# Layer 2 of a four-layer image network on one NeuronCore: three buffers in its first and last pass, ACT and PSUM in the first, and padded rows of delta*u in DRAM

## The reference

```
xc    = silu(conv3x3(x_norm @ in_proj_w[:, :C]) + conv_b);  z = the other half
xs    = [xc in row order, reversed, in column order, reversed]        # 4 directions
proj  = xs @ x_proj_w                                                 # 12 + 16 (B) + 16 (C) rows
delta = softplus(proj[:12] @ dt_w + 2 * dt_b)
state = exp(delta * A) * state + (delta * u) * B                      # per channel, 16 states, 3136 steps
y     = sum over states(state * C) + D * u
out   = x + (layernorm(sum of the 4 directions) * ln_g + ln_b) * z @ out_w
```

## Time and profile before

| what | value |
|---|---|
| time, median of 3 runs | 19143.47 us (19140.31 to 19148.17) |
| profiled execution, its own time | 19173.11 us |
| its span, first to last instruction | 19171.4 us |
| busy share PE, PEld, DVE, ACT, POOL | 78, 58, 61, 38, 36% |
| DMA | 2640.22 MB, mean 138 GB/s |
| mean granted TensorE clock | 0.794 |

### The profile page before, as it was taken

One profiled execution on the slowest core, in us unless ns is written; L12 is line 12 of the kernel. 1 busy time (PEld: TensorE's weight loads), 2 busy tenths in 40 slices (PEclk: granted clock), 3 DMA queues, 4 the chain that ended last, 5 costly groups with the idle time before them and its releaser, 6 DMA issues. The chain is left out here.

```text
span 19171.4 us, 359393 instructions
## 1 busy us (share of the span) xinstructions
PE 14991.3 (78%) x130080; PEld 11045.3 (58%) x130080; DVE 11710.9 (61%) x10632; ACT 7349.9 (38%) x12681; POOL 6928.4 (36%) x3199
## 2 busy tenths in 40 slices
PE   7899898989997534444888888888888888854489
PEld 5666666666665211122777677767777677732267
DVE  5666666666665666565667676667677667732232
ACT  4444444444443333333444444444444444411100
POOL 1000000000000233335777677767777677721100
PEclk9999999999998766676777777777777777765699
DMA  5222222222223555657999999899889999954411
GB/s 123 58 59 59 63 54 59 59 63 59 59 53 89 130 139 139 149 133 171 209 208 210 211 209 208 207 210 209 207 209 211 208 210 210 210 129 115 115 48 40
DMA packets 1692801, 2640.22 MB, mean 138 GB/s; under 512 B 1081676, under 2 KB 1245260, under 8 KB 1667404
## 3 DMA queue, kind: packets, MB, share of 16 engines
q1 hardware_dynamic: 1680332, 2551.26, 56.3%
q0 software_dynamic: 12288, 86.71, 2.1%
HBM read 2110.03 MB, written 556.32 MB: 139 GB/s over the span
## 5 line engine op out<-in xcount | busy, mean ns | idle before, releaser
L1680 DVE TENSOR_TENSOR_SCAN L2.h<-L2.ps,L2.db 128x912 f32<-128x912 f32 x2688 | 5514.0, 2056 | 2416.1 <-POOL L2.db L1545 2320.6
L1545 POOL TENSOR_TENSOR L2.db<-L2.du,L2.bt 128x896 f32<-128x896 f32 x2688 | 5576.7, 2093 | 2388.2 <-DMA L2.du<-du 2306.2
L1568 PE MATMUL L2.ps<-L2.dm,L2.wa 32*128 32x112 f32 (+2 forms) x24192 | 4522.0, 346 | 1132.1 <-DVE L2.h L1680 1005.5
L1568 PEld LDWEIGHTS L2.ps<-L2.dm,L2.wa 32*128 32x128 f32 x24192 | 4169.2, 258 | 1838.8 <-DVE L2.h L1680 1294.7
L1620 ACT ACTIVATE L2.ps<-L2.ps 128x896 f32<-128x896 f32 x2688 | 2426.0, 903 | 4607.2 <-PE L2.ps L1568 4606.8
L1580 PE MATMUL L2.ps<-L2.h,L2.cd 128*8 128x96 f32 x50176 | 2575.8, 362 | 4.2 <-DVE L2.h L1680 4.2
L1580 PEld LDWEIGHTS L2.ps<-L2.h,L2.cd 128*8 128x8 f32 x50176 | 1443.6, 108 | 583.8 <-DVE L2.h L1680 4.3
L1137 POOL TENSOR_TENSOR L2p.work<-L2p.work,L2p.xc 128x784 f32<-128x784 f32 x192 | 451.3, 2350 | 1659.2 <-DVE L2p.work L1300 1659.2
L314 POOL TENSOR_TENSOR L1.x_res<-L1.x_res,L1.ob 96x3136 f32 (+1 forms) x16 | 95.4, 5976 | 2584.8 <-ACT L1.qv L457 2584.8
L366 PE MATMUL L1.p_proj<-L1.xt,L1.w_hi 128*96 128x448 f32 x3024 | 826.9, 383 | 194.3 <-DVE L1.xt L560 167.4
L366 PE MATMUL L0.p_proj<-L0.xt,L0.w_hi 128*96 128x448 f32 x3024 | 824.2, 382 | 193.9 <-DVE L0.xt L560 167.4
(11 more groups left out here) (242 smaller groups left out, 20801.6 us busy)
## 6 DMA issues: line engine op xcount, KB each, us to landing
L2.du<-du SPq DMA_DIRECT2D x2688, 448.0 KB, 11.1
L2.dm<-d SPq DMA_DIRECT2D x896, 336.0 KB, 10.8
du<-L2p.work SPq DMA_DIRECT2D x128, 784.0 KB, 7.6
y<-L2.ysum SPq DMA_DIRECT2D x896, 84.0 KB
L0.left<-table SPq DMA_DIRECT2D x48, 1176.0 KB
L0.right<-table SPq DMA_DIRECT2D x48, 1176.0 KB
L1.left<-table SPq DMA_DIRECT2D x48, 1176.0 KB
L1.right<-table SPq DMA_DIRECT2D x48, 1176.0 KB
```

Of the source, the lines that this page charges most:

```text
L1545: pool.tensor_tensor(db[:, n % RB, :, 2:ROW], du[:, n % RD, :].rearrange("p (c t) -> p c t", t=SPAN), row, ALU.mult)\
L1568: mm = pe.matmul(decays[n % RA][:, a:b], wa[rows, j, :], dm[rows, j, a - lo:b - lo], start=True, stop=True)
L1680: dve.tensor_tensor_scan(h[:, half, u * UNIT:(u + 1) * UNIT, :].rearrange("p c t -> p (c t)"), decays[n % RA], db[:, n % RB, :, :].rearran ...
```

## The change

In `prep_layer`: `one` and `d` get a third buffer, which lies in `xn` parts 0 and 1, and `hi` a second, in `xn` part 2. `one_of(n)` and `d_of(n)` choose by (n + 1) % 3, `hi_of(n)` by (n + 1) % 2. ACT's logarithm writes to `ln_out`, one buffer of two PSUM banks, so that logarithm q waits for DVE's subtraction of q - 1; the copy to hi moves from DVE to ACT, between the logarithms. The next pair's `load_x` moves from before the tiles to after the stores of tile 10, and waits until they have landed. In `fin_layer`: three buffers; SP loads only y, as soon as the turns of the chunk three before are done, and ahead of the stores; ACT issues the loads of xc, z and x; PE's order becomes `skips(i + 1)`, `turns(i)`, `shares(i - 1)`, and DVE's `total(i + 1)`, `gate(i)`, `add_out(i - 1)`. In DRAM each (image, copy) of `du` becomes one flat row with `UNIT * SPAN` = 896 floats behind it, 3584 bytes; its stores and loads address the same data in it. The semaphores and counts follow.

```diff
+        ones = [work[:, (1 + s) * TOK:(2 + s) * TOK] for s in range(2)] + [xn[:, 0, :]]
+        ds = [work[:, (3 + s) * TOK:(4 + s) * TOK] for s in range(2)] + [xn[:, 1, :]]
+        his = [hi[:], xn[:, 2, :].bitcast(F32R)]
         pads = [v.rearrange("p (h w) -> p h w", w=PADDED)
                 for v in (pad0[:], work[:, TOK:TOK + PADDED * PADDED], work[:, 3 * TOK:3 * TOK + PADDED * PADDED])]
...
-        def d_stores(n, step=1):
+        def one_of(n):
+
+            return ones[(n + 1) % 3]
+
+        def d_of(n):
+
+            return ds[(n + 1) % 3]
+
+        def hi_of(n):
+
...
-                    sp.wait_ge(d_step, 2 * q)
+                    sp.wait_ge(hi_done, q)
                     for run in set_runs(pr, i):
-                        store_part(0, hi[:].bitcast(F32), *run).then_inc(hi_stored[half], 16)
+                        store_part(0, hi_of(n).bitcast(F32), *run).then_inc(hi_stored[n % 2][half], 16)
                     sp.wait_ge(du_done, q)
                     for at, b, c, size in runs(pr, i):
                         for copy in range(COPIES):
-                            sp.dma_start(du_dram[k, b, copy, spans, c:c + size, :].rearrange("s c t -> c s t"),
-                                         one[n % 2][at:at + size, span].rearrange("p (s t) -> p s t", t=SPAN))\
-                                .then_inc(du_stored[n % 2][half], 16)
+                            rows = du_dram[k, b, copy, 0:NSPANS * CH * SPAN].rearrange("(s c t) -> c s t", c=CH, t=SPAN)
+                            sp.dma_start(rows[c:c + size, spans, :],
+                                         one_of(n)[at:at + size, span].rearrange("p (s t) -> p s t", t=SPAN))\
+                                .then_inc(du_stored[n % 3][half], 16)
                     sp.wait_ge(lo_done, q)
                     for run in set_runs(pr, i):
-                        store_part(1, d[n % 2], *run).then_inc(lo_stored[n % 2][half], 16)
+                        store_part(1, d_of(n), *run).then_inc(lo_stored[n % 3][half], 16)
             load_x(0)
...
-                if pr + 1 < PAIRS:
-                    load_x(pr + 1)
                 for i in range(3):
...
                         store_rows(pr, j // 3 + 1)
+                    if j == TILES - 2 and pr + 1 < PAIRS:
+                        n = pr * TILES + j
+                        for half in range(2):
+                            sp.wait_ge(hi_stored[n % 2][half], d_stores(n + 2, 2))
+                            sp.wait_ge(lo_stored[n % 3][half], d_stores(n + 3, 3))
+                            sp.wait_ge(du_stored[n % 3][half], du_stores(n + 3, 3))
+                        load_x(pr + 1)
...
-                    if n >= 2 and q % 2 == 0:
-                        act.wait_ge(lo_stored[n % 2][q // 2], d_stores(n, 2))
+                    if n >= 3 and q % 2 == 0:
...
             def log(pr, j):
                 n = pr * TILES + j
+
+                def split(q):
+                    act.wait_ge(d_step, 4 * n + q + 1)
+                    if n >= 2 and q % 2 == 0:
+                        act.wait_ge(hi_stored[n % 2][q // 2], d_stores(n, 2))
+                        act.wait_ge(lo_done, 4 * (n - 2) + q + 2)
+                    act.copy(hi_of(n)[:, piece(q)], d_of(n)[:, piece(q)]).then_inc(hi_done, 1)
+
                 for q in range(4):
                     act.wait_ge(s_step, 12 * n + 3 * q + 2)
-                    act.activation(one[n % 2][:, piece(q)], one[n % 2][:, piece(q)], ACT.Ln).then_inc(ln_done, 1)
+                    if n or q:
+                        act.wait_ge(d_step, 4 * n + q)
+                    act.activation(ln_out, one_of(n)[:, piece(q)].rearrange("p (a n) -> p a n", a=2), ACT.Ln)\
+                        .then_inc(ln_done, 1)
+                    if q:
+                        split(q - 1)
+                split(3)
             for pr in range(PAIRS):
                 act.wait_ge(step, pr * STEPS + 9)
...
                 for q in range(4):
-                    o_q, d_q = (v[n % 2][:, piece(q)] for v in (one, d))
+                    d_q = d_of(n)[:, piece(q)].rearrange("p (a n) -> p a n", a=2)
                     dve.wait_ge(ln_done, 4 * n + q + 1)
                     dve.wait_ge(s_step, 12 * n + 3 * q + 3)
-                    dve.scalar_tensor_tensor(out=d_q, in0=o_q, scalar=ln1[:], in1=d_q, op0=ALU.subtract,
+                    dve.scalar_tensor_tensor(out=d_q, in0=ln_out, scalar=ln1[:], in1=d_q, op0=ALU.subtract,
                                              op1=ALU.add).then_inc(d_step, 1)
-                    dve.wait_ge(d_step, 8 * n + 2 * q + 1)
-                    if n and q % 2 == 0:
-                        dve.wait_ge(hi_stored[q // 2], d_stores(n))
-                        dve.wait_ge(lo_done, 4 * (n - 1) + q + 2)
-                    dve.tensor_copy(hi[:, piece(q)], d_q).then_inc(d_step, 1)
             def conv(pr, i):
...
             def load_du(k, s, half, u):
                 c = half * HALF + u * UNIT
-                rows = du_dram[k].rearrange("b o s c t -> (b o) s (c t)")
+                rows = du_dram[k, :, :, 0:NSPANS * CH * SPAN].rearrange("b o (s n) -> (b o) s n", s=NSPANS)
...
-        yk = m.sb("yk", [SPAN, 2, DIRS, LINES, CH])
...
+        NS = 3
+        yk = m.sb("yk", [SPAN, NS, DIRS, LINES, CH])
...
                                 sp.dma_start(place_e[SIDE * a:SIDE * a + SIDE], src).then_inc(y_in[s], 16)
-                span = slice(t * CHUNK, (t + 1) * CHUNK)
-                sp.dma_start(xc[:, s, :, :], xc_dram[pr, :, :, span]).then_inc(xc_in[s], 16)
-                sp.dma_start(zc[:, s, :, :], z_dram[pr, :, :, span]).then_inc(fin_in[s], 16)
-                for out, src in image_parts(x_in, pr, lambda i: xr[:, s, i, :], t * CHUNK, CHUNK):
-                    sp.dma_start(out, src).then_inc(fin_in[s], 16)
-
-            load(0)
-            load(1)
-            for n in range(NC):
-                s = n % 2
+
+            def store(n):
                 sp.wait_ge(out_done, n + 1)
-                for src, dst in image_parts(x_out, n // NCHUNK, lambda i: oc[:, s, i, :], n % NCHUNK * CHUNK, CHUNK):
-                    sp.dma_start(dst, src).then_inc(x_stored[s], 16)
-                if n + 2 < NC:
-                    load(n + 2)
-            for s in range(2):
-                sp.wait_ge(x_stored[s], 64 * NC // 2)
+                for src, dst in image_parts(x_out, n // NCHUNK, lambda i: oc[:, n % NS, i, :], n % NCHUNK * CHUNK, CHUNK):
+                    sp.dma_start(dst, src).then_inc(x_stored[n % NS], 16)
+
+            for n in range(NS):
+                load_y(n)
+            for i in range(NC + 1):
+                if i + NS < NC:
+                    sp.wait_ge(turned, 3 * (i + 1))
+                    load_y(i + NS)
+                if i:
+                    store(i - 1)
+            for s in range(NS):
+                sp.wait_ge(x_stored[s], 64 * len(range(s, NC, NS)))
         @block.gpsimd
         def _(pool):
             for n in range(NC):
...
             skips(0)
-            for n in range(NC):
-                turns(n)
-                if n + 1 < NC:
-                    skips(n + 1)
-                shares(n)
+            for i in range(NC + 1):
+                if i + 1 < NC:
+                    skips(i + 1)
+                if i < NC:
+                    turns(i)
+                if i:
+                    shares(i - 1)
...
+            def load_xc(n):
+                pr, t = divmod(n, NCHUNK)
+                if n >= NS:
+                    act.wait_ge(skip_ready, (n - NS + 1) * (LINES // 2))
+                act.dma_start(xc[:, n % NS, :, :], xc_dram[pr, :, :, t * CHUNK:(t + 1) * CHUNK]).then_inc(xc_in[n % NS], 16)
+
+            def load_z(n):
+                pr, t = divmod(n, NCHUNK)
+                if n >= NS:
+                    act.wait_ge(gated, n - NS + 1)
+                act.dma_start(zc[:, n % NS, :, :], z_dram[pr, :, :, t * CHUNK:(t + 1) * CHUNK]).then_inc(z_in[n % NS], 16)
+
+            def load_x(n):
+                if n >= NS:
+                    act.wait_ge(out_done, n - NS + 1)
+                for out, src in image_parts(x_in, n // NCHUNK, lambda i: xr[:, n % NS, i, :], n % NCHUNK * CHUNK, CHUNK):
+                    act.dma_start(out, src).then_inc(xr_in[n % NS], 16)
+
+            for n in range(NS):
+                load_xc(n)
+            for n in range(2):
+                load_z(n)
...
+            for i in range(NC):
+                scale(i)
+                if i + 1 < NC:
+                    normalise(i + 1)
+                if i + NS < NC:
+                    load_xc(i + NS)
+                if i + 2 < NC:
+                    load_z(i + 2)
+                if i + 1 < NC:
+                    load_x(i + 1)
         @block.vector
...
+            def gate(n):
+
+                s = n % NS
                 dve.wait_ge(scaled, 3 * n + 3)
-                dve.wait_ge(fin_in[s], 80 * (n // 2 + 1))
+                dve.wait_ge(z_in[s], 16 * (n // NS + 1))
```

(24 more changed lines are left out.)

106 lines of the change are left out of this document (53 added, 53 removed).

## The result

| | before | after |
|---|---|---|
| median | 19142.56 us (4 runs, 19140.31 to 19148.17) | 18094.31 us (4 runs, 18079.56 to 18105.79) |
| ratio | | 0.9451, 95% interval 0.9438 to 0.9463 |
| profiled execution | 19173.11 us | 18079.56 us |
| first pass | 2724.7 | 2303.1 |
| scan | 7952.0 | 7952.2 |

A stage is counted here from its first DMA on the SP queue (the first pass from its second, the load of `w_gn`) to the next stage's first. So counted, the last pass took 1344.9 us before; the 1375 of the earlier trace rows reach 30 us into layer 3. The change brings 1048 us (5.5%); forecast were 1090.

The account below looks back on a forecast made before the run. Stores alternating with arithmetic were taken to bound the first pass, a circle of loads, work and stores the last; in the scan DMA was 0.90 busy. Terms -450 - 640 + 0 = -1090 gave 18050 us, range 16950 to 18450.

Parts of the forecast that it names:

- First pass, -450 forecast: First pass of layer 2: a direction falls from 134.2 to 104 us, 16 times, less 30 for the moved load.
- The step from the stores to ACT's order: First pass: with third buffers, stores need 86 us a direction, ACT's program order 104, so ACT becomes the bound.
- factor 16: First pass: the gain per direction, 134.2 - 104 us, counted for all 16 directions, 483 us.
- load of `x`: First pass, pair changes: the later load is mostly covered by tile 11's arithmetic; 10 us per pair, 30 in all.
- the 3.00 of my upper end: First pass: DVE's subtraction at 3.00 us beside POOL instead of 1.03, giving 128 us a direction.
- Last pass, -640 forecast: Last pass: three buffers and the new order overlap loads with work, a chunk falls from 49.1 to 25 us.
- lower end of 21.6 us a chunk: Last pass: DMA bound if the clock rises with denser PE work, 735 us off.
- that rule alone: Last pass: issuing from more engines saves only issuing time, 4.6 us a chunk, 130 us in all.
- Scan, 0 forecast: Scan: the changed pitch of du has no effect, 35.5 us a half span and 209 GB/s stay; chance 0.60.
- padding works: Rival, chance 0.25: in the scan the pad lifts du loads from 271 to 387 GB/s, 960 us off, 17090 in all.
- padding hurts: Rival, chance 0.04: in the scan the pad drops du loads to 203 GB/s, 1520 us on, 19570 in all.
- the lone unit's 387 GB/s: Scan: one du load alone at the old pitch reaches 387 GB/s, so its aligned rows do not collide.

Follow-up runs that it names:

- spreading the copies: Copies to f, with PE's projections, dealt out in pairs around the soft parts of two tiles, against the changed kernel: 17947.3 us, first pass 2163.0.
- distinct pieces: Scan loads of delta*u read 128 different DRAM pieces instead of 16 pieces 8 times each, against the changed kernel: 18038.5 us, scan 7906.0.

## Why the prediction was right, and where it wasn't

**The whole.** 18050 was forecast, 18094 came, inside the range. In the profiled executions the stages give -421.6 + 0.2 - 669.2 = -1090.6, against -1090; the medians differ by 1048, since the profiled execution of before lay 30 us above its median and that of after 15 us below. That the stages' sum met the forecast within 1 us is luck: the first pass brought 28 us less than forecast and the last 29 more.

**First pass, -450 forecast, -421.6 measured.** The step from the stores to ACT's order as the bound was right, and spreading the copies showed it. The direction came out at 100.3 instead of 104: soft 11.0 as in the earlier trace rows, log 10.7 without the long wait (10.2 forecast), copies 28.2 (25), and waits of 2 x 3.8 instead of 15. (134.2 - 100.3) x 16 would be 542 off, 120 more than came. Two terms were mis-sized.

The first is the **factor 16**. A pair has two such intervals, not four, and six tiles more. In its first interval the fall was 6.9 us in the mean of the four pairs, where two tiles at 33.9/3 us each would give 22.6: in the kernel before, Relu of tiles 0 and 1 of a pair never waited, since the last pair's stores had landed, so a third buffer had nothing to take away there (all 868.8 us lie in tiles 2 to 11). That is 4 x 15.7 = 63 us. The last four tiles of the pass, up to the scan, did come out at full value, 181.8 to 136.2 us.

The second is the **load of `x`**. The same four tiles with a change of pairs behind them got only 27.0 us shorter, not 45.6. If the rest of the change is as before, the moved load costs 18.6 us there, an estimate from these intervals: 56 in all, instead of the 10 us and 30 that I took, and inside the 0 to 20 that I had allowed. Against the kernel with two buffers and the early load the same sum gives 18.2 us (292.3 - 271.1 = 21.2 for the interval, 175.6 - 136.2 = 39.4 at the end). The step set the load against tile 11's arithmetic. But the stores run more than 20 us behind it (DVE done at 7312.1, tile 10's last store issued until 7333), so the cover was over before the load began. The 45 us that DVE idles are more than this cost: late stores hold the next pair back through the pads as well, and with the early load ACT waits 41.41 us for them at the same place. Against the forecast, -63 and -26 were partly covered by +59 from the period (3.7 us x 16): the 28 us by which the pass missed are small by luck.

**PSUM and ACT's cast.** 1.03 us beside POOL was right; with two SBUF operands it was 1.6 in the mean, not the 3.00 of my upper end, and 61 us the price. The cast on ACT, which my text took as relief for DVE, brings nothing and by one run costs 12 us. The third buffers make 401 of the 422 us, the moved load's cost already taken off.

**Last pass, -640 forecast, -669 measured.** The overlap came as described. The 49.1 us a chunk before held 30 us of the next layer; the outputs were 48.1 us apart. A chunk now took 22.7 us instead of 25: PE's work fell from 23.8 to 584.57/28 = 20.9 us as the clock rose from 0.59 to 0.71, which is near the lower end of 21.6 us a chunk that I had named. In ten chunks of the middle PE is busy 0.92 of the time and DMA share is 0.91; which of the two sets the 22.7 us no run shows. Against the 640, the smaller chunk before and the faster one after partly cancel: a chunk gained 48.1 - 22.7 = 25.4 us where 49.1 - 25 = 24.1 were forecast. The second queue, in which the prediction saw 130 us at most by that rule alone, is worth none.

**Scan, 0 forecast.** The two profiled executions agree (7952.0 and 7952.2) and would have closed the case, too early: that of before lay 30 us above its median. Nine profiled scans with the pad and the usual loads took 7951 to 7992 us, 7966 in the mean; without it 7917 and 7904, besides the 7952 of before. Run against run the pad costs about 50 us, 0.3%. So "padding works" is excluded, "padding hurts" has the sign but a thirtieth of its 1520 us, and this one term is as large as the 44 us between forecast and result. I had taken 0 because the lone unit's 387 GB/s spoke against colliding rows. It did, against large effects; neither the pad nor distinct pieces bring the stage's mean rate above 210 GB/s, and a small cost of the wrong sign was beyond what that row could tell.

## What to carry to other kernels

Third buffers are worth what the queue wait says only as far as the next bound in the written order: add up one engine's program for a period before pricing them. Before multiplying a gain per period, count the periods in which the wait really occurs; here the first two tiles of every outer iteration had none. When a buffer is borrowed from data that the next iteration loads, price that load from where the store queue stands, not from where the arithmetic stands. A layout edit that "can't hurt" wants its own comparison of several runs; one profile of each hides 50 us in 18000.

## What was not expected of the hardware

A DVE instruction on 112 x 8 values took 2.44 us where it takes 0.17 in the kernel with two buffers in the last pass, whose POOL has long been done by then, and it ended at 16908.93, with POOL's sum (16905.47 + 3.43 = 16908.90). This is no accident of one chunk: in 24 of the 28 chunks POOL's sum was running when it began; it then took 0.22 to 3.22 us and ended 25 to 31 ns after POOL's instruction each time. In the four others it took 0.17. So DVE waited for POOL to finish, however small its own work.

The f32 cast on DVE also depends on POOL. In the kernel before, the 44 casts that began while POOL was idle, 0.1 us ahead of its next instruction, took 0.57 us, and the 148 that began while POOL was at work took 2.09, which gives the mean of 1738 ns in the earlier trace rows.

And the loads of 16 rows were slower in both of the other layouts tried: with 3584 bytes more per row by some 50 us of scan, at 4 MiB by some 200 us more than that.
